# First choice's rows weighed by VectorE, routing roots by Newton's method, statistics and six shared parts moved, in a macaron block with mixture-of-experts FFNs

## The reference

```python
def _layernorm(x, axis=-1, eps=1e-05):
    m = jnp.mean(x, axis=axis, keepdims=True)
    v = jnp.var(x, axis=axis, keepdims=True)
    return (x - m) / jnp.sqrt(v + eps)
...
# gate: 16 experts in 4 groups, 2 groups kept, 2 experts chosen
scores = jax.nn.softmax(xf @ gate_w.T); orig = scores
scores = scores + gate_b
...
weights = jnp.take_along_axis(orig, idx, axis=1)
...
h = jax.nn.silu(xf @ We1 + be1) * (xf @ We3 + be3)          # per expert
y = sum over the two chosen experts of weight * (h @ We2 + be2)
z = jax.nn.silu(xf @ ws1 + bs1) * (xf @ ws3 + bs3) @ ws2 + bs2   # shared expert
return y + z
...
x = x + 0.5 * ffn(layernorm(x))
x = x + linear_attention(layernorm(x))   # relu(q), relu(k), 16 heads, then a projection
x = x + 0.5 * ffn(layernorm(x))
```

## Time and profile before

| what | us |
|---|---|
| runs | 1244.09, 1245.39, 1242.54; median 1244.09 |
| the profiled execution | 1243.24, span 1241.5 |
| PE busy | 1148.4 (93%) |
| DVE busy | 852.7 (69%) |
| ACT busy | 759.6 (61%) |
| POOL busy | 698.1 (56%) |
| chain that ended last | PE 58%, DVE 17%, ACT 11%, issue 5%, POOL 5%, DMA 3% |

### The profile page before, as it was taken

How to read it: one execution, slowest core, us unless ns; L and a number is a source line. 1 busy time by engine, 2 the same in 40 slices (tenths; PEclk the granted TensorE clock), 3 DMA queues, 4 the chain that set the end, 5 groups by cost and what they waited for, 6 DMA issues and landing times.

```text
span 1241.5 us, 26349 instructions
## 1 busy us (share of the span) xinstructions
PE 1148.4 (93%) x6696; PEld 904.6 (73%) x6696; DVE 852.7 (69%) x2774; ACT 759.6 (61%) x1698; POOL 698.1 (56%) x850
## 2 busy tenths in 40 slices
PE   7988999999999967899998999889998999999995
PEld 5555555899999946777887878545557999999653
DVE  6788784566666655768878786677844666666488
ACT  4454441688888845675655653544415888888398
POOL 3577776488888854000411503356763888887810
PEclk9999999999999998999999999899999999999997
DMA  9922227556555523012320400114585555555398
GB/s 360 309 91 95 98 104 201 172 172 174 171 172 156 164 104 105 32 38 68 112 72 24 133 22 35 35 69 141 171 210 180 173 170 174 173 157 162 119 400 333
DMA packets 94215, 181.53 MB, mean 146 GB/s; under 512 B 17624, under 2 KB 60400, under 8 KB 92022
## 3 DMA queue, kind: packets, MB, share of 16 engines
q1 hardware_dynamic: 66630, 110.44, 29.2%
q0 software_dynamic: 26016, 67.55, 15.3%
q10 hardware_dynamic: 1424, 1.86, 0.5%
HBM read 97.63 MB, written 86.08 MB: 148 GB/s over the span
## 4 chain that ended last, share of the span: by engine, by line
PE 58%; DVE 17%; ACT 11%; issue 5%; POOL 5%; DMA 3%; SPq 1%; DVEq 0%; ACTq 0%; POOLq 0%
PE bank L700 20%; PE bank L710 10%; PE bank L559 7%; PE bank L691 5%; POOL expert_rows L1683 4%; PE bank L575 4%; PE bank L806 3%; ACT rows L1021 3%; ACT w L1021 3%; DVE stat L1161 2%; PE bank L756 2%; PE bank L732 2%; ACT xn L1039 1%; PE bank L521 1%; ACT rows L898 1%
## 5 line engine op out<-in xcount | busy, mean ns | idle before, releaser
L700 PE MATMUL bank<-rows,att 128*128 128x128 f32 x2288 | 303.2, 276 | 0.3 <-ACT att L1010 0.3
L700 PEld LDWEIGHTS bank<-rows,att 128*128 128x128 f32 x2288 | 279.2, 192 | 0.8 <-ACT att L1010 0.6
L1683 POOL DMA_INDIRECT expert_rows<-rows,slots x160 | 155.4, 971 | 80.0 <-issue 57.3
L1010 ACT COPY att<-w 128x512 f32 x286 | 177.0, 619 | 10.2 <-issue 4.2
L1740 POOL DMA_INDIRECT routed_rows<-silu,rdest x160 | 158.3, 989 | 35.0 <-issue 24.6
L1458 DVE SCALAR_TENSOR_TENSOR rows<-bank,tile_b,att 128x128 f32<-128x128 f32 x286 | 100.1, 350 | 112.9 <-ACT att L1015 102.0
L710 PE MATMUL bank<-w,rows 128*128 x572 | 171.5, 382 | 4.3 <-DVE rows L1458 4.2
L1740 POOL DMA_INDIRECT routed_rows<-rows,rdest x126 | 124.7, 990 | 68.4 <-DVE rdest L1441 40.7
L1009 ACT COPY rows<-bank 128x256 f32<-128x256 f32 x286 | 106.6, 373 | 89.1 <-PE bank L691 86.9
L575 PE MATMUL bank<-ws,be 128*128 128x256 f32 x512 | 124.0, 388 | 8.6 <-DVE be L1364 8.6
L925 ACT ACTIVATE silu<-bank,bs 128x512 f32<-128x512 f32 x64 | 43.9, 686 | 127.6 <-PE bank L559 117.5
(11 more groups left out here) (212 smaller groups left out, 2156.9 us busy)
## 6 DMA issues: line engine op xcount, KB each, us to landing
rows<-expert_rows SPq DMA_DIRECT2D x286, 129.5 KB
rows<-routed_rows SPq DMA_DIRECT2D x32, 512.0 KB, 4.2
w<-routed_rows SPq DMA_DIRECT2D x10, 1024.0 KB, 10.9
out<-xres SPq DMA_DIRECT2D x16, 512.0 KB, 9.3
xres<-in_x SPq DMA_DIRECT2D x7, 1024.0 KB, 9.5
rows<-routed_rows SPq DMA_DIRECT2D x6, 1024.0 KB, 7.7
expert_rows<-pad SPq DMA_DIRECT2D x47, 129.5 KB, 14.0
w<-in_w SPq DMA_DIRECT2D x1, 4096.0 KB, 24.4
```

The source lines that it names most:

```text
L700: last = nc.tensor.matmul(rh_ps[t % RB][:, n * P:(n + 1) * P], m.rw13[:, t % RB, c * C + n * INTER:c * C + (n + 1) * INTER], m.rT[:, t % R ...
L1010: nc.scalar.copy(m.rw13[:, a % RB, :].rearrange("p (c n) -> p c n", c=KC), w13[:, :, bass.ds(expert_at(i + 2), C)]).then_inc(s.rw13_copied, 1)
L1683: nc.gpsimd.indirect_dma_start(out=d.xg, out_offset=bass.IndirectOffsetOnAxis(ap=m.slots[:, slots_of(r), k, i:i + 1], axis=0), in_=m.xs[bu ...
```

## The change

1. `rooted_by_dve(r)`: for r = 3 to 7 and 14, 15 DVE computes the reciprocal root itself: a first guess from the bits of `ve` (shift, then magic number minus half), and three Newton rounds of three instructions, the last of which is finished in `negate_mean`. POOL keeps the roots of the other rounds and those of attention, and the calls for these seven leave its queue. The steps counted for a window go from 17 + 4 to 17 + 7 where there are statistics.
2. `weigh` on ACT multiplies k = 1 only. DVE adds k = 0 with one `scalar_tensor_tensor` of 128x256 for each tile, (y0 * weight) + x, as soon as the rows have been loaded, and then waits for ACT's k = 1 and adds that as before.
3. Six instead of three of layer 0's shared parts are held, all of them batch 7's. In the border DVE mixes them with the combines, and ACT weighs all of batch 0 after the first three of its six parts.
4. The statistics of r = 13 move from the end of attention batch 7 to its start, behind those of r = 11, with a semaphore of their own, `later_stats`.

```diff
--- before.py
+++ after.py
@@ -137,6 +137,11 @@
     m.ve = sb("ve", [P, NT])
     m.rstd = sb("rstd", [P, NT])
     m.nmr = sb("nmr", [P, NT])
+    m.half_bits = sb("half_bits", [P, NT], I32)
+    m.root_bits = sb("root_bits", [P, NT], I32)
+    m.root = m.root_bits[:, :].bitcast(FP32)
+    m.root_by = sb("root_by", [P, NT])
+    m.root_err = sb("root_err", [P, NT])
     m.mx = sb("mx", [P, NT])
     m.sm = sb("sm", [P, NT])
     m.rs = sb("rs", [P, NT])
@@ -245,10 +250,10 @@
 PARTS = 6 * BATCHES + 1
 LEAD = (0, EARLY)
 FIRST = ((0, 4, 9, 13, 18, 22, 27, 31, 36), (0, 3, 7, 12, 16, 21))
-HELD = ((44, 46, 48), (29, *range(31, PARTS)))
+HELD = ((41, 43, 44, 45, 46, 48), (29, *range(31, PARTS)))
 TAIL = tuple(tuple(n for n in range(FIRST[L][-1], PARTS) if n not in HELD[L]) for L in range(LAYERS))
-UPS, DOWNS = (4 * 7 + 2, 4 * 13), (PAIRS * 7 + 2, PAIRS * 13)
-HELD_UP, HELD_DOWN = ((7, 2), (13, 0)), ((7, 1), (13, 0))
+UPS, DOWNS = (4 * 7, 4 * 13), (PAIRS * 7, PAIRS * 13)
+HELD_UP, HELD_DOWN = ((7, 0), (13, 0)), ((7, 0), (13, 0))
 BIASED = (7, 6, 5, 0, 1, 2, 3, 4)
 
 
@@ -289,6 +294,10 @@
 
 
 NEXT = BATCHES + EARLY
+
+
+def rooted_by_dve(r):
+    return 3 <= r < BATCHES or r > NEXT + 2
 
 
 def early_in(b, step):
@@ -322,6 +331,7 @@
     s.weights_in, s.experts_in, s.att_weights_in = sem("ffn_weights_in"), sem("experts_in"), sem("att_weights_in")
     s.spare_out, s.setup_done = sem("spare_out"), sem("setup_done")
 
+    s.later_stats = sem("later_stats")
     s.stats_ready, s.rstd_ready, s.nmr_ready = sem("stats_ready"), sem("rstd_ready"), sem("nmr_ready")
     s.xn_half, s.xT_ready, s.xT_copied = sem("xn_half"), sem("xT_ready"), sem("xT_copied")
     s.scores_ready, s.scores_copied = sem("scores_ready"), sem("scores_copied")
@@ -1016,10 +1026,9 @@
                                              bias=m.tile_b13[:, 0, i:i + 1]).then_inc(s.rsilu_ready, 1)
 
             def weigh(b, tiles, y):
-                for k in range(2):
-                    for j, i in enumerate(tiles):
-                        last = nc.scalar.activation(y[:, k, j * C:(j + 1) * C], y[:, k, j * C:(j + 1) * C], ACT.Copy,
-                                                    scale=m.weights[:, b, k, i:i + 1])
+                for j, i in enumerate(tiles):
+                    last = nc.scalar.activation(y[:, 1, j * C:(j + 1) * C], y[:, 1, j * C:(j + 1) * C], ACT.Copy,
+                                                scale=m.weights[:, b, 1, i:i + 1])
                 return last
 
             def weigh_routed(b, h):
@@ -1085,11 +1094,12 @@
             act.wait_ge(s.weights_in, 16 * len(ffn_loads))
             route(0)
             experts(0)
-            for n in HELD[0]:
+            for n in HELD[0][0:3]:
                 shared(0, n)
-
             for h in range(PAIRS):
                 weigh_routed(0, h)
+            for n in HELD[0][3:]:
+                shared(0, n)
             a_normalise(0, range(NT))
             for n in range(4):
                 a_copy_xT(0, n)
@@ -1168,6 +1178,25 @@
                 ch.then(last)
                 nc.vector.tensor_scalar(own.ve[:, :], own.mv[:, :, 1], LN_EPS, None, ALU.add).then_inc(ready, 1)
 
+            def error_of_root():
+                ch.then(TT(m.root_by[:], m.root, m.ve[:], ALU.mult))
+                ch.then(nc.vector.scalar_tensor_tensor(m.root_err[:], m.root_by[:], -0.5, m.root, ALU.mult, ALU.mult))
+
+            def better_root(out):
+                return nc.vector.scalar_tensor_tensor(out, m.root_err[:], 1.5, m.root, ALU.add, ALU.mult)
+
+            def approach_root(ready):
+                dve.wait_ge(s.stats_ready, ready)
+                ch.then(nc.vector.tensor_scalar(m.half_bits[:], m.ve[:].bitcast(I32), 1, None, ALU.arith_shift_right))
+                ch.then(nc.vector.tensor_scalar(m.root_bits[:], m.half_bits[:], -1.0, float(0x5f3759df), ALU.mult,
+                                                ALU.add))
+                for _ in range(2):
+                    error_of_root()
+                    ch.then(better_root(m.root))
+                    yield
+                error_of_root()
+                yield
+
             def route_stats(r):
                 b = r % BATCHES
                 if r < BATCHES:
@@ -1179,8 +1208,12 @@
 
             def negate_mean(r):
                 own = tiles_of(r)
-                dve.wait_ge(s.rstd_ready, r + 1)
-                wait(dve, s.xn_half, normalised_of(r))
+                if rooted_by_dve(r):
+                    wait(dve, s.xn_half, normalised_of(r))
+                    ch.then(better_root(own.rstd[:, :]))
+                else:
+                    dve.wait_ge(s.rstd_ready, r + 1 - 5 * (r >= BATCHES))
+                    wait(dve, s.xn_half, normalised_of(r))
                 nc.vector.scalar_tensor_tensor(own.nmr[:, :], own.mv[:, :, 0], -1.0, own.rstd[:, :], ALU.mult,
                                                ALU.mult).then_inc(s.nmr_ready, 1)
                 dve.wait_ge(s.nmr_ready, r + 1)
@@ -1223,6 +1256,8 @@
                     yield
                 aggregate(s.stats_ready)
                 yield
+                if rooted_by_dve(r):
+                    yield from approach_root(r + 1 - (r > NEXT + 2))
 
             def copy_scores(r):
                 dve.wait_ge(s.scores_ready, r + 1)
@@ -1365,7 +1400,7 @@
                                                ALU.add, ALU.mult).then_inc(s.gated_ready, 1)
 
             def add_shared(r, p):
-                if r == BATCHES - 1 and p == 2:
+                if r == BATCHES - 1 and p == 0:
                     dve.wait_ge(s.bias_added, 1)
                 if r == 2 * BATCHES - 3 and p == 0:
                     dve.wait_ge(s.bias_added, BATCHES + 3)
@@ -1414,7 +1449,7 @@
                     shared(L, n, work, (3 if b > LEAD[L] + 1 else 0) + 1 + ahead)
                     others = end - n - 1
                     for j in range(others):
-                        shared(L, n + 1 + j, work, (17 + 4 * ahead) // others + 1)
+                        shared(L, n + 1 + j, work, (17 + 7 * ahead) // others + 1)
                     for _ in work:
                         pass
                 work = table_work(L)
@@ -1471,13 +1506,22 @@
                             dve.wait_ge(s.rows_out[last_user % SLOTS], 16 * (last_user // SLOTS) + 16)
                         TT(m.ry[(i - 2) % RYSLOTS], ry_ps[y % RB][:, 0:C], m.be2[:, bass.ds(e, C)], ALU.add).then_inc(s.ry_scaled, 1)
 
+            def weigh_and_add(b, tiles, y):
+                for j, i in enumerate(tiles):
+                    x = m.xres[:, b, i, :]
+                    last = nc.vector.scalar_tensor_tensor(x, y[:, 0, j * C:(j + 1) * C], m.weights[:, b, 0, i:i + 1], x,
+                                                          ALU.mult, ALU.add)
+                return last
+
             def combine(b, h):
                 n = PAIRS * b + h
                 y = m.ylq[:, n % YSLOTS]
                 dve.wait_ge(s.bias_added, BIASED.index(b) + 1)
                 x = x_tiles(b, 2 * h, 2)
+                dve.wait_ge(s.routed_in[n % YSLOTS], 16 * (n // YSLOTS + 1))
+                ch.did(weigh_and_add(b, range(2 * h, 2 * h + 2), y))
                 dve.wait_ge(s.weighted, n + 1)
-                ch.then(TT(x, x, y[:, 0, :], ALU.add))
+                ch.settle()
                 TT(x, x, y[:, 1, :], ALU.add).then_inc(s.combined, 1)
                 dve.wait_ge(s.combined, n + 1)
                 stats(b, range(2 * h, 2 * h + 2))
@@ -1571,13 +1615,18 @@
             dve.wait_ge(s.weights_in, 16 * len(ffn_loads))
             route(0)
             experts(0)
-            for n in HELD[0]:
-                shared(0, n, iter(()), 0)
-
-            for h in range(PAIRS):
+            for u in range(3):
+                gated(BATCHES - 1, u)
+            for h in range(2):
+                combine(0, h)
+                add_shared(BATCHES - 1, h)
+            for h in range(2, PAIRS):
                 combine(0, h)
             aggregate(s.a_stats_ready)
+            gated(BATCHES - 1, 3)
             a_negate_mean(0)
+            for p in range(2, PAIRS):
+                add_shared(BATCHES - 1, p)
             def steps(work, count):
                 for _ in range(count):
                     next(work, None)
@@ -1597,7 +1646,9 @@
                         steps(work, 1)
                     combine(b + 1, 1)
                 else:
-                    route_stats(BATCHES + EARLY)
+                    route_stats(NEXT)
+                    stats(NEXT + 2 - BATCHES, range(NT), m.early)
+                    aggregate(s.later_stats, m.early)
                 if ranked is not None:
                     steps(work, 1)
                 sum_keys(b, 0)
@@ -1640,8 +1691,6 @@
                 if ranked is not None:
                     for _ in slots(ranked):
                         pass
-                if not more:
-                    route_stats(NEXT + 2)
                 if b == 0:
                     route_stats(BATCHES)
```

(12 more changed lines are left out.)

## The result

The changed kernel takes 1254.84 us (median of four runs, 1252.30 to 1256.28) against 1244.4 for the kernel before: ratio 1.0083, 95% interval 1.0062 to 1.0104. It is slower by 10.4 where 2.8 was forecast, and 4.3 above the range's high end.

A forecast was written before the change was run, and what follows sets the result against it. Layer 0's routing was taken to be bound by POOL's last sends, themselves held by DVE's cast of batch 7's slots. Terms +2.9 - 0.5 + 0.2 - 0.3 + 0.5 = +2.8 gave 1246.9 us, range 1236.5 to 1250.5.

The forecast's parts named there:

- POOL alone can gain 2.4 and no more: Layer 0's routing: batch 7's first send, 3.4 after its cast starts, 0.98 unavoidable, can come at most 2.4 earlier.
- the 5.3 by which DVE is late: Layer 0's routing: roots on DVE and displaced selections delay batch 7's slots by 5.3; the last send moves +2.9.
- PE's tail is not last at that hand-over: Layer 0's hand-over to experts: sends end last, so three shared parts (some 10 of PE work) leaving the tail give 0.
- The roots in layer 1: Layer 1's routing: the root of r = 14 on DVE costs +2.05, the next +0.4.
- The move of the statistics: End of attention: 3.5 of statistics leave DVE's queue before ACT's mean, less 0.67 delay of the last key sums: -2.8.
- The forecast of the stretch and layer 1's routing: End of attention and layer 1's routing: moved statistics and two roots net -0.3, between -3 and +1.5.
- Attention: Attention: slower combines cost +2.0 in batches 2, 4, 6; ACT's relief gives most back: +0.2, between -1.8 and +1.5.
- The border: Between layer 0's experts and attention: six held parts just fit PE's idleness, ACT weighs less: -0.5, between -1.5 and +2.
- The final stage: Final stage: 16 pieces at 2.85 on DVE instead of 2.39, ACT's weighing no longer bounds: +0.5.
- Rival A: Layer 0's routing: POOL's roots bound, DVE takes them for nothing, -8.7 for +2.9: 1235.3; chance 0.20.
- Rival B: Combines and final stage: a weighed add of 256 columns costs 0.34, not 0.40: 1242.3; chance 0.20.
- Rival C: Border: POOL's bias adds stretch each weighed add by 2.2, from 0.40 to 0.88: 1248.8; chance 0.14.

The follow-up runs named there:

- experiment 1: Changed kernel with all seven roots back on POOL in their old places and the old step count: 1245.4 us, ratio 1.0009 to the kernel before.
- experiment 2: Changed kernel with both choices' rows weighed by ACT again and two plain adds on DVE: 1251.6 us, ratio 1.0059 to the kernel before.
- 3: Changed kernel with the statistics of r = 13 back at the end of the last attention batch: 1259.73 us, ratio 1.0123 to the kernel before.
- 4: Changed kernel with three held parts of layer 0 and the old border: 1256.15 us, ratio 1.0081 to the kernel before.
- 11: Changed kernel with one step more between shared parts in layer 0's windows that take statistics: 1254.8 us, ratio 1.0084 to the kernel before.
- experiment 6: Kernel before with only the statistics of r = 13 moved; three held parts and old border: 1239.14 us, ratio 0.9976.

## Why the prediction was wrong

The sign and the main place were right, the size not: +2.8 was forecast, +10.4 came, above the high end.

- **The step that failed** is "POOL alone can gain 2.4 and no more" with what followed from it: the slack between batch 7's cast and its first send (3.4 less the 0.98 that passes anyway, 2.4) was set off against the 5.3 by which DVE is late, and only 2.9 was left. The delay of DVE itself was forecast well (5.3; measured 5.9 at batch 5's slots, 6.0 at batch 7's ranks). But a slack must be read at the last place where the queue is fed late, and that is batch 5, where it was 0 (cast 152.41, send 153.39). From there on POOL has three batches of 20.28 to send and nothing helps. The delay passed whole, 5.8, and experiment 1 gives it back whole. This term is short by 2.9, and with the hand-over to the experts by 3.5. The sentence that PE's tail is not last at that hand-over was wrong too: in the kernel before it was, by some 1.6 (7.8 behind the last send against 6.2 now), but its price of 0 came out, since the low clock behind the longer idleness took back what the shorter tail gave.
- **The roots in layer 1** were put at 2.05 and 0.4, 2.45 together. From the ranks of r = 11 to those of r = 13 it takes 52.3 to 54.5 in the five profiles with these roots (the changed kernel, experiments 2, 3, 4, 11) and 48.5 to 50.2 in the nine without: 2 to 6, the middle near 4. So this term is short too, by 1.5 or so, which the next one hides. The window of r = 12 alone takes 26.1 to 29.3 without a root in it; what sets that spread is open.
- **The move of the statistics**: forecast -2.8, measured -3.0 (experiment 6) in a kernel without roots, and -4.9 if it is taken from the changed one. The closeness of the first is luck in part: in the traces the gain behind attention is 5.0, not 3.5, since PE also keeps its clock, and a longer window of r = 12 hid that in experiment 6. The forecast of the stretch and layer 1's routing, -0.3 against -0.9, is near because this error and that of the roots cancel. Its cost of 0.67 in batch 7 is in the trace: also without the split (experiment 2) batch 7's key sum comes 38.7 behind batch 6's, before 38.1.
- **Attention**: forecast +0.2, measured +2.8. The gain in batch 1 was right (-1.4 against -1.5). The term that was mis-sized is the combine, 0.99 against 0.90 (1.04 a batch against 0.68, three times, 1.1 more); batch 5, put at nothing, costs 0.5, as does batch 3 in experiments 1, 3 and 4 though not in the changed kernel's profile; and 0.65 in batch 7 belongs to the statistics.
- **The border**: -0.5 forecast, +0.9 measured. No part of the 0.5 came, and the last held part, which was to end within 0.2 of the first transpose, made it 2.5 late: its gated product came only behind the combines, and its 16 matmuls ran at half the clock. 1.6 of that came back.
- **The final stage**: +0.5 forecast, +2.7 measured: 0.06 a piece for 16, and 1.4 in the first piece beside POOL's adds. The excess is in one weighed add, and those behind it started 0.4 apart as ever.
- **Rival A** (POOL bounds and the roots are free) fell: its premise, unbroken sends from batch 2 on, was true, and its conclusion false, because DVE was exactly as late as POOL at batch 5. With five roots less on POOL the sends merely got gaps. **Rival B** fell: a weighed add starts 0.39 to 0.40 behind the last one, not 0.34. The Trainium skill, "VectorE: DVE Perf Modes", section "The TRN2 errata — SBUF-src ops pay a fixed extra latency per instruction", by whose formula 0.33 is the estimate for 256 columns, is not borne out here: one weighed add takes 0.48. **Rival C** was right that POOL's bias adds hold DVE, and wrong in where and how. In the border POOL's adds were over when the combines of batch 0 began, and two weighed adds took 0.87. What they held was one instruction each time and not every one by a factor: a small copy ahead of batch 1's combines (4.64 for 0.38), and in the final stage the first weighed add (1.87 for 0.48). In the border this cost next to nothing, since PE was not ready sooner.

By ratios to the kernel before the parts are: roots with the displaced selection +0.74% (experiment 1 against the changed kernel), weighing +0.24% (2), statistics -0.24% (6), held parts nothing (4, 6): 0.74% where 0.83% was measured, inside the intervals.
